# Two gated layers on one core: the first attention's values computed token by token, rearranged through DRAM, and its queries evacuated by ScalarE

## The chip, the cores and the metric

The kernel runs on one core of one Trainium2 chip. The metric is the device time of one execution in microseconds (us), less is better. A core has TensorE (PE; its weight loads are listed as PEld), VectorE (DVE), ScalarE (ACT), GpSimd (POOL), and SyncE (SP), which here issues DMAs.

## The reference, cut to what matters

Two layers follow one another. Each is `x + s * g`, where `s` is an attention and `g` a gated network on the normalised `x`. The first layer's attention works over heads, within each token: for every token the 16 query heads are compared with the 16 key heads of the same token.

```python
def _L0_attn_ref(x, w_qkv, b_qkv, w_out, b_out):
    qkv = x @ w_qkv + b_qkv
    qkv = qkv.reshape(Bq, Lq, NUM_HEADS, 3 * HEAD_DIM)      # 16 heads of 64
    q, k, v = jnp.split(qkv, 3, axis=-1)
    k = k + pos_enc[None, :, None, :]
    attn = jnp.einsum('blhd,blgd->blhg', q, k) / scale
    attn = jax.nn.softmax(attn, axis=-1)
    out = jnp.einsum('blhg,blgd->blhd', attn, v)
    return out.reshape(Bq, Lq, NUM_HEADS * HEAD_DIM) @ w_out + b_out
```

Here x is 2 sequences of 1024 tokens, 128 features wide, in fp32. The rest (the first layer's mixture of 16 experts with its router, the second layer's attention over tokens and its ternary network) is left as it is.

## The kernel before, in words

Each engine runs one instruction stream, written out in order at the end of `two_layers` (lines 2223 to 2409); semaphores tie the streams together. `first_norm` loads and normalises, `head_attention` is the stage of the change, `experts`, `second_attention` and `last_network` follow.

`head_attention` works in 8 blocks of 128 tokens (of both sequences at once) and 16 turns of 64 tokens, two turns to a block. Activations lie feature-major: features on the partitions, tokens along the free axis. In turn `i`, TensorE's stream (`tensor`, line 633) is, in this order:

- `tensor_scores`, two halves (line 558): a query-by-key product for 8 groups of 8 tokens, into banks 2 to 5;
- projection units of the next block (`tensor_project`, line 528): a block has 12 units, 4 of q, 4 of k, 4 of v, and a turn runs 6. A unit is 8 fp32 products into one of banks 0 and 1. It waits until the unit two before it has been evacuated. Turn 0 starts at unit 8, so an even turn runs v, v, v, v, q, q and an odd turn q, q, k, k, k, k. The first two units stand together, the other four alternate with
- the four quarters of `tensor_out` (line 595): the weighted sum for turn `i - 2`, from `vt` (values with (head, token) on the partitions) and `wide` (the probabilities spread over a block-diagonal);
- `tensor_values`, two halves of 4 transposes (line 577), which turn this turn's v into `vt` by way of banks 2 and 3;
- `tensor_turn` (line 586), two transposes of the probabilities of turn `i - 1`; a step of the norm or the router (`f.tensor`); and `tensor_y` (line 615), the output projection of turn `i - 2`.

VectorE masks the scores (`vector_same`, L682), evacuates q and k units (L671, L677, with bias or position added), sums ex (L720) and takes reciprocals, reduces the scores (L691) and takes the top (L731). ScalarE takes exps (L782), evacuates v units with four 128-column instructions each (L762), copies the transposed v into `vt` (L777), the sums (L770), the turned probabilities (L788) and y (L793). GpSimd subtracts the top (L848), spreads the probabilities over `wide` with four instructions for turn `i - 2` (`gpsimd_wide`, L833), scales (L857), and then, in even turns, makes `kb` for the next block (L824), in eight later turns a slice of the experts' weights' parts (L441 to L447). So the spread of turn `i - 2` stands behind the subtraction of turn `i - 1`, which waits for L731. SP only issues the loads of the start (lines 177 to 200), all at once, and waits for nothing. The two score blocks of a turn go through `sm0` and `sm1`; the last turn is written out by hand and interleaved with the experts' first products (lines 2238 to 2259).

An fp32r product takes its operands' rounded parts: the experts' matrices are products hi·hi + lo·hi + hi·lo of such parts (lines 1032 to 1038).

## Time and profile before

| | |
|---|---|
| Time, median of 3 runs | 1138.16 us (1137.54 to 1138.43) |
| The profiled execution, own time | 1136.68 us |
| its span, first to last instruction | 1134.6 us |
| granted TensorE clock, mean | 0.997 |
| head-attention turns (first scores to the experts) | about 20.8 to 232 us of the span |
| DMA in the first 28 us | 219 GB/s, 2 to 3 GB/s after that until the next stage's loads |

A profile's page gives the busy time of each engine, then slices of the span, DMA, the chain of work that ended last, and groups of instructions. The share of busy time says which engine could be the bound; the chain of waits in order of time, and the timeline of a stretch, say what a given turn waited for. A matrix product's recorded duration overlaps its neighbours', so what one costs is read from the distance between starts. One fp32 product appears as two records.

### The profile page before, as it was taken

The numbers are of one execution on the slowest core, as the hardware profiler recorded it, in microseconds if no ns is written. First come the engines' busy times: TensorE is split into PE (matmuls) and PEld (weight loads), VectorE is DVE, ScalarE is ACT, GpSimd is POOL, SyncE is SP. The second block draws the span as 40 slices with busy tenths as digits, with TensorE's granted clock in tenths as the row PEclk, the third lists the DMA queues.
The fourth block names the chain that finished last, engine by engine and source line by source line (L and its number), as shares of the span: only waits on it lengthen the run. The fifth ranks groups of instructions, "written<-read, shape, count | busy, mean of one in ns | idle before, by whom it ended". The sixth has DMA issues, their size and how long they took to land.

```text
span 1134.6 us, 22214 instructions
## 1 busy us (share of the span) xinstructions
PE 1116.5 (98%) x8936; PEld 730.3 (64%) x8936; DVE 847.5 (75%) x1251; ACT 597.8 (53%) x949; POOL 783.8 (69%) x505
## 2 busy tenths in 40 slices
PE   9999999999989999999999999999999999999998
PEld 8899999887765555555454555455455555457886
DVE  5676886657676788878788788878788887896554
ACT  2443444657656555545555555555465455654443
POOL 3666776854436888888987988988988888960000
PEclk9999999999999999999999999999999999999999
DMA  6000000020000000200000000000000000000000
GB/s 219 3 2 2 3 3 3 2 77 1 1 1 1 1 1 26 77 2 1 1 1 1 1 1 2 1 1 1 1 1 1 1 1 1 1 1 10 1 10 19
DMA packets 7686, 13.69 MB, mean 12 GB/s; under 512 B 1809, under 2 KB 5137, under 8 KB 7329
## 3 DMA queue, kind: packets, MB, share of 16 engines
q1 hardware_dynamic: 7264, 12.26, 3.3%
q8 instruction: 72, 1.18, 0.4%
q14 instruction: 30, 0.24, 0.1%
q10 hardware_dynamic: 320, 0.01, 0.0%
HBM read 11.22 MB, written 1.05 MB: 11 GB/s over the span
## 4 chain that ended last, share of the span: by engine, by line
PE 90%; DVE 6%; ACT 2%; issue 2%; POOL 0%; DVEq 0%; ACTq 0%; POOLq 0%
PE o_ps L1547 19%; PE ha_banks L553 7%; PE mx_ps L1502 7%; PE st_ps L1525 5%; PE st_ps L1531 5%; PE st_ps L1528 5%; PE bank L1943 3%; PE bank L1945 3%; PE bank L1944 3%; PE ha_banks L620 3%; PE ha_banks L573 3%; PE mx_ps L1440 3%; PE ha_banks L609 2%; PE pj_ps L1459 2%; PE pj_ps L1451 2%; DVE mx_part L1755 2%
## 5 line engine op out<-in xcount | busy, mean ns | idle before, releaser
L1857 POOL TENSOR_TENSOR acc<-acc,prob 128x1024 f32<-128x1024 f32 x192 | 468.6, 2440 | 63.0 <-ACT prob L1681 52.8
L1681 ACT ACTIVATE prob<-st_ps 128x1024 f32<-128x1024 f32 x256 | 248.5, 1023 | 208.8 <-PE st_ps L1531 208.8
L1547 PE MATMUL o_ps<-prob,v_cur 128*64 128x512 f32 x1024 | 245.6, 599 | 0.0
L1752 DVE TENSOR_REDUCE mx_part<-mx_ps 128x1 f32<-128x512 f32 x258 | 164.8, 666 | 72.4 <-PE mx_ps L1502 72.4
L1547 PEld LDWEIGHTS o_ps<-prob,v_cur 128*64 128x64 f32 x1024 | 68.0, 136 | 96.3 <-issue 77.5
L1755 DVE TENSOR_REDUCE mx_part<-mx_ps 128x2 f32<-128x1024 f32 x79 | 94.9, 1201 | 44.6 <-PE mx_ps L1502 44.6
L1771 DVE RECIPROCAL rden<-rden 128x128 f32<-128x128 f32 x128 | 120.5, 942 | 0.0
L1502 PEld LDWEIGHTS mx_ps<-k_hi,q_hi 64*128 64x128 f32 x416 | 46.7, 183 | 107.2 <-issue 95.5
L1502 PE MATMUL mx_ps<-k_hi,q_hi 64*128 64x512 f32 x416 | 112.3, 457 | 1.5 <-DVE mx_part L1755 1.3
L1531 PE MATMUL st_ps<-q_hi,d_lo 64*128 64x512 f32 x512 | 100.9, 391 | 0.0
L1857 POOL TENSOR_TENSOR acc<-prob 128x1024 f32<-128x1024 f32 x32 | 76.1, 2379 | 29.3 <-PE pj_ps L1436 18.9
L833 POOL TENSOR_TENSOR ha_wide<-ha_pt,ha_own 128x512 f32<-128x512 f32 x64 | 73.7, 1183 | 8.3 <-ACT ha_pt L788 8.3
L1525 PE MATMUL st_ps<-q_hi,d_hi 64*128 64x512 f32 x384 | 75.9, 392 | 0.0
L1528 PE MATMUL st_ps<-q_lo,d_hi 64*128 64x512 f32 x384 | 75.1, 388 | 0.0
L553 PE MATMUL ha_banks<-xn,head_wkv 128*64 128x128 f32 x1024 | 66.0, 274 | 1.6 <-DVE ha_q L671 1.0
L1752 DVE TENSOR_REDUCE mx_part<-pj_ps 128x1 f32<-128x512 f32 x86 | 58.0, 675 | 0.0
L553 PEld LDWEIGHTS ha_banks<-xn,head_wkv 128*64 128x64 f32 x1024 | 55.0, 136 | 4.6 <-DVE ha_q L671 1.4
L1531 PEld LDWEIGHTS st_ps<-q_hi,d_lo 64*128 64x128 f32 x512 | 48.2, 185 | 11.1
L2069 ACT ACTIVATE whole<-bank,cols 128x512 f32<-128x512 f32 x32 | 22.0, 688 | 62.1 <-PE bank L1945 60.1
L682 DVE TENSOR_TENSOR ha_sm<-ha_banks,ha_same 128x1024 f32<-128x1024 f32 x32 | 37.6, 1216 | 19.9 <-PE ha_banks L573 19.8
L762 ACT ACTIVATE ha_v<-ha_banks,ha_head_bv 128x128 f32<-128x128 f32 x128 | 35.6, 375 | 24.6 <-PE ha_banks L553 24.6
L1645 ACT ACTIVATE rden<-pj_ps 128x512 f32<-128x512 f32 x32 | 19.1, 598 | 53.9 <-PE pj_ps L1451 53.9
(404 smaller groups left out, 2319.3 us busy)
## 6 DMA issues: line engine op xcount, KB each, us to landing
h_w<-in_h SPq DMA_DIRECT2D x2, 1024.0 KB, 7.8
w_raw<-in_w SPq DMA_DIRECT2D x8, 192.0 KB, 3.6
head_wkv<-in_wkv SPq DMA_DIRECT2D x2, 512.0 KB, 6.3
m_w<-in_m SPq DMA_DIRECT2D x3, 256.0 KB, 2.9
out<-fin SPq DMA_DIRECT2D x3, 256.0 KB, 2.2
sel_raw<-in_sel SPq DMA_DIRECT2D x1, 576.0 KB, 10.1
head_wq<-in_wq SPq DMA_DIRECT2D x1, 512.0 KB, 4.4
x<-in_x SPq DMA_DIRECT2D x2, 256.0 KB, 7.8
```

Source lines behind the costliest of these rows:

```text
L553: mm = pe.matmul(pj_ps[n % 2][rows(seq), j, :], lhs, xn[:, seq * HALVES + b // TT, at_token:at_token + BLK], start=True, stop=True, skip_g ...
L833: d = pool.tensor_tensor(wide[r][:, seq, :, :, :], t.unsqueeze(3).to_broadcast([P, G // 2, HEADS, GROUPS]), own[:, :].unsqueeze(1).unsquee ...
L1502: mm = pe.matmul(to[h], q_hi[q % 2][rows(h), tile(i)], k_hi[q % 2][rows(h), half_of(keys)], start=True, stop=True)
L1525: pe.matmul(st[:, h, :], upper[rows(h), :], qh[rows(h), half_of(half)], start=False, stop=False, skip_group_check=True)
L1528: pe.matmul(st[:, h, :], upper[rows(h), :], ql[rows(h), half_of(half)], start=False, stop=False, skip_group_check=True)
L1531: mm = pe.matmul(st[:, h, :], dl[rows(h), tile(j)], qh[rows(h), half_of(half)], start=False, stop=True, skip_group_check=True)
L1547: mm = pe.matmul(o_ps[rows(h), :], v_cur[:, m % 2, j, rows(h)], prob[:, (16 * m + slot) % RING, h, :], start=(j == 0), stop=(j == KT - 1), ...
L1681: act.activation(prob[:, n % RING, :, :], st_ps[:, slot % 2, :, :], ACT.Exp, scale=SCALE).then_inc(s_exp, 1)
L1752: dve.reduce_max(mx_part[:, h, i, keys:keys + 1], maxima_banks(q, n)[h], AX_X).then_inc(s_mxr, 1)
L1755: dve.reduce_max(mx_part[:, :, i, keys:keys + 1], both, AX_X).then_inc(s_mxr, 1)
L1771: dve.reciprocal(part, part).then_inc(s_rcp, 1)
L1857: pool.tensor_tensor(total, old, new, ALU.add).then_inc(s_acc, 1)
```

## The change: what it does

- **Values.** A v unit is now one sequence and eight heads: 128 tokens on the output's partitions, 512 columns (head, dimension). It is three fp32r products: hi·hi, hi·lo, lo·hi, of parts of the tokens (`xv_hi` by ScalarE, `xv_lo` by GpSimd, one block at a time) and of the weights (`wv_hi` by ScalarE, the low part by GpSimd into the place of the weights, once at the start). The v units keep their places in the order.
- **Evacuation.** VectorE evacuates v, adding a bias row that is broadcast to all partitions; q goes to ScalarE, four instructions for each unit. k stays with VectorE but is written group by group, and both its inputs are now read with a step of 16 elements. VectorE evacuates the third v unit before its first reduction of an even turn, and the fourth between the two.
- **The rearrangement.** The 16 transposes of a block and their copies go. SP, once a block's four v units are out, stores v (1 MB) to DRAM, waits for the store, and loads each turn's `vt` (512 KB) in pieces of 512 bytes, behind a wait for the weighted sums of two turns before. `tensor_out` waits for that load.
- **Order of rows.** Tokens and heads are (group, head) instead of (head, group) on the partitions of `vt`; `prob` is written with another inner order, a second mask tile `mask_g` is loaded, and y is written in the new token order.
- **The start.** The bias row is first gathered, DRAM to DRAM, in 1024 pieces of 4 bytes; SP waits for it before it issues the broadcast and all the loads behind it (positions, the second half of x, `wo`, the router's and the experts' weights). The masks' loads are issued between the gather and the wait.
- **The end.** The experts' second gate product stands one step earlier; its wait is for the last masked scores.

The diff, cut to its core:

```diff
@@ -28,7 +28,7 @@
-HEAD_W = {"wo": (PAIRS, P), "bq": (2, PAIRS), "bk": (HEADS,), "bv": (HEADS,), "pos": (LEN,), "mask_h": (P,)}
+HEAD_W = {"wo": (PAIRS, P), "bq": (2, PAIRS), "bk": (HEADS,), "pos": (LEN,), "mask_h": (P,), "mask_g": (P,)}
...
@@ -184,9 +185,13 @@
+        sp.dma_start(w.bv_row, a["bkv0"][HD:P, :].rearrange("n h -> h n"), allow_slow_non_contiguous=True)\
+            .then_inc(s_row, 16)
-        for seq in range(SEQS):
-            sp.dma_start(w.bv[HD * seq:HD * seq + HD, :], a["bkv0"][HD:P, :]).then_inc(s_bv, 16)
+        sp.dma_start(w.mask_g[:, :], a["mask"]).then_inc(s_mask, 16)
+        sp.wait_ge(s_row, 16)
+        sp.dma_start(w.bv[:, :, :], w.bv_row.unsqueeze(0).to_broadcast([P, HEADS, HD])).then_inc(s_bv, 16)
...
@@ -478,12 +491,13 @@
-    q, k = zip(*((room.sb(f"q{i}", [P, BLK // G, HEADS, G]), room.sb(f"k{i}", [P, HEADS, BLK])) for i in range(2)))
-    v = room.sb("v", [P, BLK // TURN, G, HEADS, GROUPS])
+    q, k = zip(*((room.sb(f"q{i}", [P, BLK // G, HEADS, G]), room.sb(f"k{i}", [P, BLK // G, HEADS, G])) for i in range(2)))
+    v = room.sb("v", [P, HEADS, SEQS, HD])
...
-    sc, ex, prob = ([room.sb(f"{n}{i}", [P, SEQS, HEADS, GROUPS]) for i in range(2)] for n in ("sc", "ex", "prob"))
+    sc, ex = ([room.sb(f"{n}{i}", [P, SEQS, HEADS, GROUPS]) for i in range(2)] for n in ("sc", "ex"))
+    prob = [room.sb(f"prob{i}", [P, SEQS, GROUPS, HEADS]) for i in range(2)]
...
@@ -513,6 +528,32 @@
+    def grouped(t):
+        return t.rearrange("r h (t g) -> r h g t", t=G)
...
+    def value_unit(u):
+        return u % SEQS, slice((u - 2 * QU) // SEQS * PAIRS, (u - 2 * QU) // SEQS * PAIRS + PAIRS)
...
+    def over_rows(t):
+        return t[:, :, :, :].rearrange("r s g h -> r s h g")
...
@@ -529,37 +570,48 @@
-            pe.wait_ge(f.s_cur, {0: 1, 1: 2, TT: CHUNKS}[b])
+            wait_tokens(pe, b)
...
-            if u_was < 2 * QU:
-                pe.wait_ge(s_qk, b_was * 2 * QU + u_was + 1)
+            if u_was < QU:
+                pe.wait_ge(s_q, b_was * QU + u_was + 1)
+            elif u_was < 2 * QU:
+                pe.wait_ge(s_k, b_was * QU + u_was - QU + 1)
...
+        if u >= 2 * QU:
+            if u == 2 * QU:
+                pe.wait_ge(s_xvlo, b + 1)
+                if b == 0:
+                    pe.wait_ge(s_wvlo, 1)
+            seq, heads = value_unit(u)
+            hi, lo = (t[:, b % 2, seq, :] for t in (w.xv_hi, w.xv_lo))
+            to = banks[:, n % 2, :]
+            pe.matmul(to, hi, w.wv_hi[:, heads, :], start=True, stop=False)
+            pe.matmul(to, hi, w.wkv_lo[:, heads, HD:P], start=False, stop=False)
+            pe.matmul(to, lo, w.wv_hi[:, heads, :], start=False, stop=True).then_inc(s_pj, 1)
+            return
...
-            pe.wait_ge(s_qk, (i // 2 + 1) * 2 * QU)
+            pe.wait_ge(s_q, (i // 2 + 1) * QU)
+            pe.wait_ge(s_k, (i // 2 + 1) * QU)
         if half == 0 and i >= 1:
-            pe.wait_ge(s_vtc, 2 * i)
+            pe.wait_ge(s_mul, 2 * i - 1)
...
-                               k[i // 2 % 2][rows(seq), :, of * G:of * G + G], start=True, stop=True)
+                               k[i // 2 % 2][rows(seq), of, :, :], start=True, stop=True)
...
-    def tensor_values(pe, i, half):
-        if half == 0:
-            if i % 2 == 0:
-                pe.wait_ge(s_vo, (i // 2 + 1) * QU)
-            pe.wait_ge(s_mul, 2 * i + 1)
-        for t in range(G // 2):
-            mm = pe.transpose(x_ps[half][:, tile(t)], v[:, i % 2, half * G // 2 + t, :, :], c.ident[:, :])
-        mm.then_inc(s_vt, 1)
...
-            pe.wait_ge(s_vtc, 2 * n + r + 1)
+            if r == 0:
+                pe.wait_ge(s_vt[n % 2], 16 * (n // 2 + 1))
...
-        tensor_values(pe, i, 0)
-        tensor_values(pe, i, 1)
...
@@ -658,24 +700,29 @@
-        if u >= 2 * QU:
+        if u < QU:
...
-        if u < QU:
-            dve.wait_ge(s_pj, n + 1)
-            bias = w.bq[:, :, :].rearrange("r o p -> r (o p)")[:, heads].unsqueeze(2).unsqueeze(3)
-            d = dve.tensor_tensor(q[b % 2][:, :, heads, :].rearrange("r g h t -> r h g t"),
-                                  pj_ps[n % 2][:, :, :].rearrange("r h (g t) -> r h g t", t=G),
-                                  bias.to_broadcast([P, UNIT, BLK // G, G]), ALU.add)
...
-            d = dve.tensor_tensor(k[b % 2][:, heads, :], pj_ps[n % 2][:, :, :], kb[:, heads, :], ALU.add)
-        d.then_inc(s_qk, 1)
+            dve.tensor_tensor(k[b % 2][:, :, heads, :].rearrange("r g h t -> r h g t"), grouped(pj_ps[n % 2]),
+                              grouped(kb[:, heads, :]), ALU.add).then_inc(s_k, 1)
+            return
+        seq, heads = value_unit(u)
+        if n == 2 * QU:
+            dve.wait_ge(f.s_bv, 16)
+        if u == 2 * QU and b >= 1:
+            dve.wait_ge(s_vst, 16 * b)
+        dve.wait_ge(s_pj, n + 1)
+        dve.tensor_tensor(v[:, heads, seq, :], banks[:, n % 2, :].rearrange("r (h n) -> r h n", n=HD), w.bv[:, heads, :],
+                          ALU.add).then_inc(s_vo, 1)
...
-        dve.wait_ge(f.s_mask, 16)
+        dve.wait_ge(f.s_mask, 32)
-        dve.tensor_scalar(own[:, :], w.mask_h[:, 0:P:HEADS], 0.0, None, ALU.is_ge).then_inc(s_same, 1)
+        dve.tensor_scalar(own[:, :], w.mask_g[:, 0:P:HEADS], 0.0, None, ALU.is_ge).then_inc(s_same, 1)
...
-        for b, u in units(i, (2, 3, 4) if i % 2 else ()):
+        for b, u in units(i, (2, 3, 4) if i % 2 else (2,)):
...
-        for b, u in units(i, (5,) if i % 2 else ()):
+        for b, u in units(i, (5,) if i % 2 else (3,)):
...
-        for b, u in units(i, () if i % 2 else (4, 5)):
-            vector_project(dve, b, u)
...
@@ -746,22 +790,45 @@
...
-        if u < 2 * QU:
+        if u >= QU:
...
+        if n == 0:
+            act.wait_ge(f.s_bq, 16 * 2 * SEQS)
...
+        bias = w.bq[:, :, :].rearrange("r o p -> r (o p)")
-            h = u % QU * UNIT + j
-            d = act.activation(v[:, :, :, h, :], pj_ps[n % 2][:, j, :].rearrange("r (o g t) -> r o t g", t=G, g=GROUPS),
-                               ACT.Identity, bias=w.bv[:, h:h + 1])
-        d.then_inc(s_vo, 1)
+            h = u * UNIT + j
+            d = act.activation(q[b % 2][:, :, h, :], pj_ps[n % 2][:, j, :].rearrange("r (t g) -> r g t", t=G),
+                               ACT.Identity, bias=bias[:, h:h + 1])
+        d.then_inc(s_q, 1)
+    def scalar_tokens(act, b):
+        wait_tokens(act, b)
+        if b >= 2:
+            act.wait_ge(s_pj, (b - 1) * UNITS)
+        act.activation(w.xv_hi[:, b % 2, :, :], tokens_of(b), ACT.Copy).then_inc(s_xvhi, 1)
+    def scalar_begin(act):
+        scalar_tokens(act, 0)
+        scalar_project(act, 0, 0)
+        f.scalar_first_square(act, 1)
+        scalar_project(act, 0, 1)
+        scalar_project(act, 0, 2)
+        f.scalar_first_root(act, 1)
+        scalar_project(act, 0, 3)
+        wait_heads(act)
+        act.activation(w.wv_hi[:, :, :], w.wkv[:, :, HD:P], ACT.Copy).then_inc(s_wvhi, 1)
...
-    def scalar_values(act, i, half):
-        act.wait_ge(s_vt, 2 * i + half + 1)
-        act.activation(vt[i % 2][:, half * G // 2:half * G // 2 + G // 2, :].rearrange("r t n -> r (t n)"), x_ps[half],
-                       ACT.Copy).then_inc(s_vtc, 1)
...
@@ -789,28 +849,27 @@
-        tokens = c.y[:, :].rearrange("r (s b o g t) -> r s b o g t", s=SEQS, t=G, g=GROUPS, o=BLK // TURN)
-        act.activation(tokens[:, :, n // 2, n % 2, :, :].rearrange("r s g t -> r t s g"),
+        tokens = c.y[:, :].rearrange("r (s b t o g) -> r s b o t g", s=SEQS, t=G, g=GROUPS, o=BLK // TURN)
+        act.activation(tokens[:, :, n // 2, n % 2, :, :].rearrange("r s t g -> r t s g"),
...
-        for b, u in units(i, (0, 1, 2, 3)):
+        for b, u in units(i, (0, 1) if i % 2 else ()):
             scalar_project(act, b, u)
+        if i % 2 and i // 2 + 1 < BLOCKS:
+            scalar_tokens(act, i // 2 + 1)
-        for b, u in units(i, (4, 5)):
+            scalar_out(act, i - 2, 1)
+        for b, u in units(i, () if i % 2 else (4,)):
             scalar_project(act, b, u)
-        if i >= 2:
-            scalar_out(act, i - 2, 1)
-        scalar_values(act, i, 0)
-        scalar_values(act, i, 1)
         if i >= 1:
             scalar_turned(act, i - 1)
+        for b, u in units(i, () if i % 2 else (5,)):
+            scalar_project(act, b, u)
...
@@ -835,10 +894,35 @@
+    def gpsimd_tokens(pool, b):
+        pool.wait_ge(s_xvhi, b + 1)
+        if b >= 2:
+            pool.wait_ge(s_pj, (b - 1) * UNITS)
+        pool.tensor_tensor(w.xv_lo[:, b % 2, :, :], tokens_of(b), w.xv_hi[:, b % 2, :, :].bitcast(F32), ALU.subtract)\
+            .then_inc(s_xvlo, 1)
+    def sync(sp):
+        for b in range(BLOCKS):
+            sp.wait_ge(s_vo, (b + 1) * QU)
+            sp.dma_start(w.v_rows[b], v[:, :, :, :].rearrange("r h s n -> r (h s n)")).then_inc(s_vst, 16)
+            sp.wait_ge(s_vst, 16 * (b + 1))
+            by_turn = w.v_rows[b].rearrange("(t o g) (h n) -> o (g h) t n", t=G, g=GROUPS, n=SEQS * HD)
+            for o_turn in range(BLK // TURN):
+                n = b * (BLK // TURN) + o_turn
+                if n >= 2:
+                    sp.wait_ge(s_o, 2 * (n - 2) + 2)
+                sp.dma_start(vt[n % 2][:, :, :], by_turn[o_turn]).then_inc(s_vt[n % 2], 16)
...
+        gpsimd_tokens(pool, 0)
+        pool.wait_ge(s_wvhi, 1)
+        pool.tensor_tensor(w.wkv_lo[:, :, HD:P], w.wkv[:, :, HD:P], w.wv_hi[:, :, :].bitcast(F32), ALU.subtract).then_inc(s_wvlo, 1)
...
-            pool.tensor_tensor(prob[n % 2][:, :, :, :], ex[n % 2][:, :, :, :], over_heads(rtotal[n % 2]), ALU.mult)\
+            pool.tensor_tensor(over_rows(prob[n % 2]), ex[n % 2][:, :, :, :], over_heads(rtotal[n % 2]), ALU.mult)\
+        if i % 2 and i // 2 + 1 < BLOCKS:
+            gpsimd_tokens(pool, i // 2 + 1)
...
-            pe.wait_ge(head.s_vtc, 2 * head.TURNS)
+            pe.wait_ge(head.s_mul, 2 * head.TURNS)
...
@@ -2169,6 +2256,13 @@
+        w.wv_hi = room.sb("head_wv_hi", [P, HEADS, HD], F32R)
+        w.wkv_lo = Region(nc, XR + 4 * KB).sb("head_wkv_lo", [P, HEADS, P], F32R)
+        w.bv = room.sb("head_bv", [P, HEADS, HD])
+        w.xv_hi, w.xv_lo = (room.sb(n, [P, 2, SEQS, P], F32R) for n in ("head_xv_hi", "head_xv_lo"))
+        w.v_rows = nc.dram_tensor("v_rows", (LEN // P, P, SEQS * HEADS * HD), F32, kind="Internal").ap()
+        w.bv_row = nc.dram_tensor("bv_row", (HEADS, HD), F32, kind="Internal").ap()
...
+                head.sync(sp)
...
@@ -2240,12 +2335,10 @@
-                head.tensor_values(pe, TURNS - 1, 0)
-                head.tensor_values(pe, TURNS - 1, 1)
+                e.tensor_gates(pe, 1)
...
-                e.tensor_gates(pe, 1)
...
+                head.scalar_begin(act)
```

## Rows read from the trace of the kernel before

**Rows 1.** The page's first part: busy time of each engine, share, instructions.

```profile
PE 1116.5 (98%) x8936; PEld 730.3 (64%) x8936; DVE 847.5 (75%) x1251; ACT 597.8 (53%) x949; POOL 783.8 (69%) x505
```

**Rows 2.** Chain of waits in order of time, 0 to 330: start, duration (us), work.

```profile
110.45 1.99 PE ha_banks L573 x32
...
122.74 1.99 PE ha_banks L573 x32
...
135.19 1.99 PE ha_banks L573 x32
```

**Rows 3.** Timeline, 107 to 134, weight loads: start, duration, engine, line, out<-in, count.

```profile
119.64 0.86 PEld L583 LDWEIGHTS ha_banks<-ident,ha_v 128*128 128x128 f32 x8 [0.17 <-issue]
...
120.46 0.25 PEld L592 LDWEIGHTS ha_banks<-ident,ha_prob 128*128 128x128 f32 x2
...
122.67 1.86 PEld L573 LDWEIGHTS ha_banks<-ha_k,ha_q 64*128 64x128 f32 x32
...
124.65 1.73 PEld L553 LDWEIGHTS ha_banks<-xn,head_wkv 128*64 128x64 f32 x32
...
126.34 0.60 PEld L609 LDWEIGHTS ha_banks<-ha_wide,ha_vt 128*64 128x64 f32 x16
...
127.05 0.85 PEld L553 LDWEIGHTS ha_banks<-xn,head_wkv 128*64 128x64 f32 x16
...
128.38 0.86 PEld L553 LDWEIGHTS ha_banks<-xn,head_wkv 128*64 128x64 f32 x16
```

**Rows 4.** Timeline, 198 to 250, matrix products, where fp32r and fp32 products meet.

```profile
213.07 0.49 PE L1036 MATMUL g_ps<-xm_hi,wg_hi 128*128 128x512 f32 x1
...
213.40 0.39 PE L1037 MATMUL g_ps<-xm_hi,wg_lo 128*128 128x512 f32 x1
...
214.66 1.15 PE L609 MATMUL ha_banks<-ha_wide,ha_vt 128*64 128x64 f32 x32
```

**Rows 5.** Timeline, 107 to 134, VectorE and GpSimd at a turn's change.

```profile
122.06 0.61 DVE L731 TENSOR_REDUCE ha_top<-ha_sc 128x16 f32<-128x256 f32 x1
...
123.44 4.72 POOL L833 TENSOR_TENSOR ha_wide<-ha_pt,ha_own 128x512 f32<-128x512 f32 x4
```

**Rows 6.** Groups by line and form: busy us, mean ns, idle before them.

```profile
L682 DVE TENSOR_TENSOR ha_sm<-ha_banks,ha_same 128x1024 f32<-128x1024 f32 x32 | 37.6, 1216 | 19.9 <-PE ha_banks L573 19.8
...
L677 DVE TENSOR_TENSOR ha_k<-ha_banks,ha_kb 128x512 f32<-128x512 f32 x32 | 21.6, 675 | 9.4 <-PE ha_banks L553 9.2
...
L731 DVE TENSOR_REDUCE ha_top<-ha_sc 128x16 f32<-128x256 f32 x16 | 10.0, 622 | 0.6
...
L377 DVE TENSOR_REDUCE ha_top<-ha_lg 128x16 f32<-128x256 f32 x1 | 0.4, 407 | 0.0
...
L762 ACT ACTIVATE ha_v<-ha_banks,ha_head_bv 128x128 f32<-128x128 f32 x128 | 35.6, 375 | 24.6 <-PE ha_banks L553 24.6
...
L1857 POOL TENSOR_TENSOR acc<-acc,prob 128x1024 f32<-128x1024 f32 x192 | 468.6, 2440 | 63.0 <-ACT prob L1681 52.8
```

**Rows 7.** DMA: queue (packets, MB, share of 16 engines); issues (KB, us to landing).

```profile
q1 hardware_dynamic: 7264, 12.26, 3.3%
...
head_wq<-in_wq SPq DMA_DIRECT2D x1, 512.0 KB, 4.4
...
out<-fin SPq DMA_DIRECT2D x3, 256.0 KB, 2.2
...
ha_head_bq<-in_bq ACTq DMA_DIRECT2D x4, 2.0 KB, 3.2
```

**Rows 8.** Timeline, first turns: the masks, and the first weighted sum.

```profile
20.67 0.25 DVE L696 TENSOR_SCALAR ha_same<-ha_head_mask_h 128x128 f32<-128x128 f32 x1
...
45.11 0.69 PE L609 MATMUL ha_banks<-ha_wide,ha_vt 128*64 128x64 f32 x16 [0.60 <-issue]
```

**Rows 9.** Timeline, 198 to 250: the weighted sum of turn 14.

```profile
220.54 1.15 PE L609 MATMUL ha_banks<-ha_wide,ha_vt 128*64 128x64 f32 x32
```

71 lines of the change are left out of this document (38 added, 33 removed).

## The prediction

> **What bounds the kernel now.** I read the page's busy times first. TensorE is busy 98% of the span [rows 1], so only what leaves TensorE's stream, or holds it up, moves the end. The chain of waits in order of time then shows the stage that is changed: scores follow scores at 110.45, 122.74 and 135.19 us, so an odd turn takes 12.29 us and an even one 12.45 [rows 2]. Last the timeline of the even turn that begins at 122.67 [rows 3] splits it: scores 1.98 (to 124.65), the first two v units 1.69 (to 126.34), a unit and a quarter of the weighted sum together 1.33 (127.05 to 128.38), the eight transposes 0.82 (119.64 to 120.46, in the turn before), and the turned probabilities with the output projection 2.21 (to 122.67). Of the 0.71 between 126.34 and 127.05 a quarter needs 0.53; the rest, 0.18, is a wait for a v evacuation. TensorE is back to back; the others run behind it. What matters is how close.
>
> **What the change removes.** The transposes go: 0.82 us a turn, 16 turns, 13.1 us at most [rows 3]. The 32 copies to `vt` go from ScalarE, which wasn't late.
>
> **What the new product costs.** In a later stretch six fp32r products of 512 columns stand between fp32 ones: 213.07 to 214.66, 1.59 us; the first takes 0.33, because it follows another kind of product, the other five 0.25 each with the change back at the end [rows 4]. So the first pair of v units (six products) costs 1.59 for 1.69 now, and a lone unit of three 0.33 + 2 × 0.25 = 0.83 for 1.69 / 2 = 0.85. Three fast products in place of eight slow ones save 0.1 us a block: nothing.
>
> **The steady even turn, walked.** Time 0 is its scores' start.
> - The odd turn before is 0.82 shorter. Its last VectorE step, the top, doesn't follow: it hangs on the last k unit, which TensorE makes before the transposes stood. Now the top ends at 122.06 + 0.61 = 122.67, at time 0 [rows 5]; then at 0.82.
> - GpSimd's spread began 0.77 after that and takes 4.72, its first half 2.36 [rows 5]: ready at 0.82 + 0.77 + 2.36 = 3.95. TensorE wants it at 1.98 + 1.59 = 3.57. A new stall of 0.38. It exists because the cover was the transposes.
> - VectorE has masked both halves (2 × 1.22 [rows 6]) by about 3.6 (its start, 1.2, is the end of the first half of the scores), and takes v units in 0.68 each (as a k unit now, 675 ns [rows 6]): first out at 4.3, TensorE wants its bank at 3.95 + 0.53 = 4.5. Third and fourth: out at about 6.6 and 8.5 (behind the sums and the first reduction), wanted at about 7.3 and 8.7. No stall, but 0.2 of slack.
> - ScalarE's q units cost four instructions, as v units did, at 375 ns [rows 6], and start later in an even turn; their banks are wanted only in the next turn. In an odd turn it does them first thing after the exps. Hidden by the copies that left. Rounding tokens and subtracting them (256 elements) are small, at places where ScalarE and GpSimd wait.
> - So an even turn changes by −0.82 − 0.10 − 0.18 + 0.38 = −0.7, an odd one by −0.82. Turns 3 to 14 are six of each: **−9.1 us**.
>
> **The last turn.** Its transposes stood where TensorE waited for the probabilities of VectorE; the moved gate product covers the same wait. Saved: 0. But the last `vt` load is due early, see below.
>
> **The DRAM trip.** Store 1 MB: a 256 KB store landed in 2.2 us [rows 7], so between 2.2 and 8.8; load 512 KB: `head_wq` took 4.4 [rows 7]; in 512-byte pieces it may be more. 3.3% of 16 engines' 1134.6 us over 7264 packets is 0.08 us a packet [rows 7], and 64 pieces an engine are 5.3 us and landing. I take 6 and 6, with 1.2 for two issues: v complete at 8.5, `vt` at about 22. It is due at 11.75 + 11.47 + 3.95 = 27.2. Hidden, with 5 us of slack; without that cover each us too late is paid in each of 7 blocks. For the last block no projection lies between: turn 14's sum ran at 220.54 [rows 9], 22.1 after its scores, and would now be due at 21.4. Ready at 8.5 + 2.2 + 4.4 + 1.2 = 16.3 at best, 24 at worst: 0 to 2.6 us, I take 0.5.
>
> **The start.** SP now waits for the gather of 1024 pieces, 64 an engine: at 0.08 each, 5 us [rows 7], behind the weights in the same queues. All later loads slide by as much; then VectorE's first v evacuation waits for the broadcast row, and GpSimd must make the weights' low part (1024 columns, 2.4 us by [rows 6]) before the first v unit. I put 1.6 us on the first two turns, which uses up their two lots of transposes. The first round trip is queued behind the weights: turn 2's sum, at 45.11 now [rows 8], may wait 0 to 4 us; I take 1.3, of which 0.82 is paid by turn 2's transposes: +0.5.
>
> **Sum.** −9.1 + 0.5 + 0.5 = −8.1: the profiled execution's 1136.68 becomes 1128.6. The median is 1.48 above it, so 1130.1; I say **1130**. By the ends of the unknown costs, 1128.5 to 1135.
>
> **Rivals.**
> - *The step of 16.* VectorE's k evacuation reads two operands with long steps. The same reduction of 256 elements takes 622 ns with a step of 8 elements (L731) and 407 without (L377) [rows 6]: 0.84 ns an element, 0.43 us a k unit, four in each odd turn. Against it: L696 reads 128 elements with a step of 16 in 0.25 us [rows 8], no longer than its size asks. If it bites, two of the four delays reach the top (the others hide in the 1.3 between units), so the spread starts 0.85 later, the stall is 1.2, and everything VectorE does in the even turn slides: even turns end 0.2 above now instead of 0.7 below. 1130 + 6 × 0.9 = **1135.5**. The Trainium skill says so too (SBUF — State Buffer, Door 1: The DMA port swizzle): accesses that cross to a new 16-byte line pay a penalty, so fp32 strides above 4 aren't free; by that rule this rival holds, and L731 agrees with it while L696 doesn't.
> - *The scores run faster.* 16 score products take 1.98, 16 products of a unit pair 1.69 [rows 3]. If the 0.29 comes from k's scattered reading, contiguous k gives it back, 14 times: **1126**. For it: the same columns. Against: scores also follow another kind of product, as in [rows 4].
> - *The gather holds SP* (slower). Four tiny loads of 2 KB took 3.2 us with at most 4 pieces an engine [rows 7], so a piece could cost up to 0.8 us when it isn't overlapped. The masks stand behind the gather and are used at 20.67 [rows 8]. The queues are free at about 14; above 0.1 us a piece the masks are late, us for us. At 0.3: 14 + 19 = 33, 12 late, **1142**. For it: each piece is a DRAM read and write of its own. Against: 0.08 is the mean of packets of 1.7 KB.
> - *The round trip is late in each block* (slower). It decides from 18.7 us after v is complete. If 512-byte pieces cost twice the mean packet and the store 8.8, `vt` comes at about 30, 3 late, 7 times: **1150**.
> - *The change doesn't do what it says:* no such case here; the transposes are gone from the stream.
>
> **How the numbers follow.** Forecast 0.45, step of 16 0.25, faster scores 0.12, gather 0.10, late round trip 0.08. A measurement of this kernel can tell 0.2% (2.3 us) from no change: below 1135.9 is faster, above 1140.4 slower. The forecast and the faster scores are faster (0.57), the step of 16 lies on the edge, half to each (0.12 and 0.13); of the two slower rivals 0.02 end within. Faster 0.69, same 0.15, slower 0.16. The range takes in the first three cases and the near part of the gather: 1125 to 1140.
>
> **What would show it.** Right: scores 11.5 us apart in odd turns and about 11.7 in even ones; a stall of 0.4 before an even turn's first sum, released by GpSimd's spread; v units 1.59 a pair; 675 ns for L677's successor; `vt`'s load released 4 or 5 us before its use. Wrong: a k evacuation near 1.1 us (step of 16); scores below 1.9; VectorE's masks or the sums waiting for a DMA; a stall of TensorE on a v unit's evacuation, which my slack of 0.2 us doesn't exclude.

## The result, and the profile after

The changed kernel takes 1141.68 us (median; 1140.52 to 1142.95) against 1138.43 for the kernel before on the same chip (1136.99 to 1141.55): a ratio of 1.0025, 95% interval 1.0014 to 1.0037. It is slower by about 3 us where 8 us of gain were forecast, and lies outside the range of 1125 to 1140. The profiled execution took 1140.92 us, 4.24 above the one of before, with a span of 1139.1, 4.5 above. It is one execution of nine, and its mean granted clock was 0.996, that of the eight others 0.992 or 0.993. The traces of e2 and e4, whose other turns are as long to 0.2 us save turns 5 and 6, have 0.992, and there turn 10 takes 18.04 and 17.74 instead of 16.74. So most executions lose more to the clock than the trace read here.

The page's first part of the changed kernel answers to [rows 1]. TensorE is busy 8.0 us less, and the span is 4.5 longer: TensorE now waits.

```profile
PE 1108.5 (97%) x8392; PEld 709.3 (62%) x8392; DVE 858.0 (75%) x1251; ACT 583.4 (51%) x926; POOL 792.0 (70%) x514
```

Where the time went is read from the starts of the turns' scores, in the chain of waits in order of time (start, duration, work), which answers to [rows 2] (in a timeline the same start can stand 0.07 earlier):

```profile
23.65 1.18 PE ha_banks L625 x16
...
44.51 2.06 PE ha_banks L625 x32
...
112.67 1.99 PE ha_banks L625 x32
...
124.19 1.99 PE ha_banks L625 x32
...
127.78 1.25 issue
...
137.15 1.99 PE ha_banks L625 x32
...
153.49 2.34 DVE ha_sm L729 x2
155.83 0.61 DVE ha_v L724
156.48 0.70 PE ha_banks L594
...
165.42 1.99 PE ha_banks L625 x32
...
213.26 1.99 PE ha_banks L625 x32
```

The turns' lengths in the two timelines, from one start of the scores to the next, and in the three experiments that matter most (us):

| turn | before | after | e5 | e7 | e9 |
|---|---|---|---|---|---|
| first scores start at | 20.81 | 23.65 | 24.43 | 20.75 | 21.62 |
| 0 and 1 together | 19.75 | 20.86 | 19.91 | 19.29 | 19.37 |
| 2 | 14.88 | 14.65 | 14.64 | 14.64 | 14.64 |
| 5 and 6 together | 28.33 | 28.30 | 29.89 | 28.49 | 29.89 |
| 7, 9 (odd) | 12.29 | 11.52 | 11.52 | 11.53 | 11.52 |
| 4, 8, 12 (even), mean | 12.75 | 12.82 | 12.13 | 12.23 | 12.11 |
| 10 | 12.73 | 16.74 | 16.13 | 14.07 | 12.10 |
| scores of turn 15 start at | 210.00 | 213.19 | 211.36 | 203.89 | 204.04 |
| span | 1134.6 | 1139.1 | 1136.4 | 1130.2 | 1129.4 |

Three things read at once. Turns 7, 9, 11 and 13 are 0.77 shorter, close to the forecast. Even turns gain nothing on the whole: 4 and 12 are 0.17 and 0.13 shorter, 8 is 0.51 longer. Two places lose much: the start, 3.95 by the scores of turn 2, and turn 10, 4.01.

The groups by line and form of the first 240 us, which answer to [rows 6]: k's read-out takes 1032 ns where it took 675; q, v, the masks and the maximum take what they were expected to.

```profile
L653 PE MATMUL ha_banks<-ha_wide,ha_vt 128*64 128x64 f32 x1024 | 41.0, 225 | 6.7 <-issue 6.6
...
L729 DVE TENSOR_TENSOR ha_sm<-ha_banks,ha_same 128x1024 f32<-128x1024 f32 x32 | 37.6, 1214 | 16.0 <-PE ha_banks L625 15.9
...
L810 ACT ACTIVATE ha_q<-ha_banks,ha_head_bq 128x128 f32<-128x128 f32 x128 | 35.8, 384 | 26.2 <-PE ha_banks L605 26.2
...
L714 DVE TENSOR_TENSOR ha_k<-ha_banks,ha_kb 128x512 f32<-128x512 f32 x32 | 32.9, 1032 | 13.8 <-PE ha_banks L605 13.8
...
L724 DVE TENSOR_TENSOR ha_v<-ha_banks,head_bv 128x512 f32<-128x512 f32 x32 | 20.9, 674 | 2.0 <-PE ha_banks L596 2.0
...
L777 DVE TENSOR_REDUCE ha_top<-ha_sc 128x16 f32<-128x256 f32 x16 | 9.9, 622 | 0.6
```

The timeline of the even turn that starts at 124.12, VectorE, GpSimd and TensorE, which answers to [rows 5]:

```profile
125.07 0.62 DVE L777 TENSOR_REDUCE ha_top<-ha_sc 128x16 f32<-128x256 f32 x1
...
126.70 2.34 DVE L729 TENSOR_TENSOR ha_sm<-ha_banks,ha_same 128x1024 f32<-128x1024 f32 x2
...
126.45 4.73 POOL L892 TENSOR_TENSOR ha_wide<-ha_pt,ha_own 128x512 f32<-128x512 f32 x4
...
129.03 0.69 PE L653 MATMUL ha_banks<-ha_wide,ha_vt 128*64 128x64 f32 x16 [1.25 <-issue]
```

The maximum ends at 125.69, 1.57 after the scores' start (forecast: 0.82), GpSimd's spread starts at 2.33 and has its first half done about 2.4 later, and TensorE, ready at 127.78, stands still for 1.25 until 129.03. Over the stage the waits before weighted sums come to 6.6 us in 7 places; before they were 0.6 in one. One of the seven, 1.10, stands in the last turn, where the moved gate product no longer fills it.

Turn 10, the timeline of VectorE and TensorE. The router's steps of turn 9 (L412 to L419) hold VectorE until 153.5, then come both masks and only then the v units; TensorE's third v unit needs a bank whose read-out stands behind all of it, and waits 2.41:

```profile
151.22 1.05 DVE L417 TENSOR_SCALAR ha_mask<-ha_rep 128x256 f32<-128x256 f32 x1
152.30 1.26 DVE L419 TENSOR_TENSOR ha_wt<-ha_mask,ha_pr 128x256 f32<-128x256 f32 x1
153.49 2.34 DVE L729 TENSOR_TENSOR ha_sm<-ha_banks,ha_same 128x1024 f32<-128x1024 f32 x2
155.75 1.27 DVE L724 TENSOR_TENSOR ha_v<-ha_banks,head_bv 128x512 f32<-128x512 f32 x2
...
156.48 0.70 PE L594 MATMUL ha_banks<-head_wv_hi,head_xv_hi 128*128 128x512 f32 x1 [2.41 <-DVE ha_v L724]
156.97 0.63 PE L595 MATMUL ha_banks<-head_wkv_lo,head_xv_hi 128*128 128x512 f32 x1
```

Before the change the same router steps stood in the same place (timeline of VectorE, kernel before), but no read-out that TensorE waits for came behind the masks:

```profile
148.46 1.03 DVE L407 TENSOR_SCALAR ha_mask<-ha_rep 128x256 f32<-128x256 f32 x1
149.53 1.27 DVE L409 TENSOR_TENSOR ha_wt<-ha_mask,ha_pr 128x256 f32<-128x256 f32 x1
150.72 2.34 DVE L682 TENSOR_TENSOR ha_sm<-ha_banks,ha_same 128x1024 f32<-128x1024 f32 x2
```

The third v unit's products then take up to 0.70 and 0.63 where others take 0.50 and 0.40. The table by stretch of the changed kernel shows the clock behind it (busy us of PE, PEld, DVE, ACT, POOL, each with its count; granted clock; DMA share; GB/s). In 152 to 156 TensorE worked 0.95 us of 4; behind that its clock is 0.58, that is, mostly the 1.2 GHz level instead of 2.4:

```profile
12.00:16.00 4.00, 3.98 (x58) 3.72 (x56) 0.37 (x2) 3.38 (x12) 0.53 (x1) 1.00 0.02 5
16.00:20.00 4.00, 2.77 (x40) 2.22 (x38) 1.60 (x2) 1.77 (x5) 2.15 (x1) 1.00 0.00 0
...
98.00:102.00 4.00, 4.00 (x32) 3.78 (x32) 0.05 (x1) 0.58 (x2) 4.00 (x5) 0.57 0.00 0
...
152.00:156.00 4.00, 0.95 (x18) 0.58 (x16) 3.97 (x5) 0.00 (x0) 3.71 (x4) 1.00 0.02 4
156.00:160.00 4.00, 3.52 (x21) 2.50 (x22) 3.62 (x6) 0.53 (x1) 2.02 (x3) 0.58 0.00 0
```

The same table has the start: from 12 to 20 us the DMA engines move next to nothing. The masks' loads have landed by 12.3, and SyncE queues nothing else: it waits for the gather, and issues the next load at 19.14. In the table of the kernel before, the same two stretches moved 262 and 386 GB/s:

```profile
12.00:16.00 4.00, 3.98 (x58) 3.64 (x54) 2.15 (x4) 0.97 (x2) 0.52 (x1) 1.00 0.98 262
16.00:20.00 4.00, 4.00 (x63) 3.49 (x61) 3.06 (x5) 0.00 (x0) 0.00 (x0) 1.00 1.02 386
```

The changed kernel's table also has a second drop of the clock, 0.57 in 98 to 102, with TensorE busy all the time.

The round trip, from the DMA issues (KB, us from issue to landing), which answers to [rows 7]: 3.9 and 4.0, and no wait for it shows in a steady turn.

```profile
v_rows<-ha_v SPq DMA_DIRECT2D x8, 1024.0 KB, 3.9
ha_vt<-v_rows SPq DMA_DIRECT2D x16, 512.0 KB, 4.0
```

### The profile page after: what moved, and what is told of

It is laid out like the page before. It is cut to its first block, busy times and chain, and to the rows that moved or that the text cites. A ratio compares the mean times of both kernels' runs of the same rounds, so it can differ in the third digit from the quotient of the medians.

```text
span 1139.1 us, 21143 instructions
## 1 busy us (share of the span) xinstructions
PE 1108.5 (97%) x8392; PEld 709.3 (62%) x8392; DVE 858.0 (75%) x1251; ACT 583.4 (51%) x926; POOL 792.0 (70%) x514
## 4 chain that ended last, share of the span: by engine, by line
PE 89%; DVE 7%; issue 2%; ACT 2%; POOL 0%; DVEq 0%; ACTq 0%; POOLq 0%
PE o_ps L1634 19%; PE mx_ps L1589 7%; PE st_ps L1612 5%; PE st_ps L1615 5%; PE st_ps L1618 5%; PE ha_banks L605 5%; PE bank L2030 3%; PE bank L2031 3%; PE bank L2032 3%; PE ha_banks L653 3%; PE mx_ps L1527 3%; PE ha_banks L664 2%; PE pj_ps L1546 2%; PE ha_banks L625 2%; PE pj_ps L1538 2%
## 5 line engine op out<-in xcount | busy, mean ns | idle before, releaser
L837 ACT ACTIVATE ha_o<-ha_banks 128x512 f32<-128x512 f32 x32 | 19.2, 599 | 69.7 <-PE ha_banks L653 69.7
L810 ACT ACTIVATE ha_q<-ha_banks,ha_head_bq 128x128 f32<-128x128 f32 x128 | 35.8, 384 | 26.2 <-PE ha_banks L605 26.2
L653 PE MATMUL ha_banks<-ha_wide,ha_vt 128*64 128x64 f32 x1024 | 41.0, 225 | 6.7 <-issue 6.6
```

The costliest lines, as they stand in the source:

```text
L653: mm = pe.matmul(o_ps[r][rows(odd), t, seq, :], vt[n % 2][:, r * G // 2 + t, rows(seq)], wide[r][:, seq, t, PAIRS * odd:PAIRS * odd + PAIR ...
```

## The experiments

All ratios are to the kernel before, run in turns on the same chip; the changed kernel stands at 1.0025. The experiments ran on four chips (e1 to e4, e5 to e8, e9, e10 and e11), so two of them are compared by their ratios. The profile shows one execution of each, and some of the effects below are smaller than what one differs from the next: the first k product starts anywhere from 14.60 to 15.85 in the thirteen traces.

**e1: k laid out plainly, scores read with a step.**

```diff
-    q, k = zip(*((room.sb(f"q{i}", [P, BLK // G, HEADS, G]), room.sb(f"k{i}", [P, BLK // G, HEADS, G])) for i in range(2)))
+    q, k = zip(*((room.sb(f"q{i}", [P, BLK // G, HEADS, G]), room.sb(f"k{i}", [P, HEADS, BLK])) for i in range(2)))
-                               k[i // 2 % 2][rows(seq), of, :, :], start=True, stop=True)
+                               k[i // 2 % 2][rows(seq), :, of:BLK:BLK // G], start=True, stop=True)
-            dve.tensor_tensor(k[b % 2][:, :, heads, :].rearrange("r g h t -> r h g t"), grouped(pj_ps[n % 2]),
-                              grouped(kb[:, heads, :]), ALU.add).then_inc(s_k, 1)
+            dve.tensor_tensor(k[b % 2][:, heads, :], pj_ps[n % 2][:, :, :], kb[:, heads, :], ALU.add).then_inc(s_k, 1)
```

> The changed kernel with k laid out as before the change: VectorE takes it out with plain runs, and the scores read the eight tokens of a group 16 apart. Result unchanged. Theory A (VectorE's 1.03 us for each k unit makes the maximum of an odd turn late, the spread weights late, and TensorE waits 1.25 us before the first weighted sum of each even turn): a k unit takes 0.68 us, the waits named issue before the sums shrink from 6.6 us to under 2, the scores stay at 2.0 us a turn, each even turn from turn 2 on is 0.7 to 1.2 us shorter, and the kernel is 5 to 8 us faster than the changed one, about 1133 to 1136. Rival B (the read-out is not on the path and the gain of TensorE is lost elsewhere): the k units are shorter, but the waits before the sums stay and the time is within 1 us of 1141.7. Rival C (the step only moves): the scores' own products get longer by more than 0.3 us a turn, and the kernel is as slow as the changed one or slower.

Measured: 1154.28 us, ratio 1.0139 (1.0110 to 1.0167). Rival C. The k units took 688 ns, as A and C say, but the score products, in the groups by line, grew from a mean of 283 to 396 ns, 1.7 us a turn:

```profile
L625 PE MATMUL ha_banks<-ha_k,ha_q 64*128 64x128 f32 x512 | 59.8, 396 | 0.4 <-issue 0.4
```

A step costs TensorE's moving operand too, and there it is on the path. The run says nothing on A: turns of 13.2 us hide any wait.

**e2: the step on the writing side.** VectorE reads in runs and writes element by element, 128 elements apart, since the groups of `k` lie 16 heads times 8 tokens apart.

```diff
-            dve.tensor_tensor(k[b % 2][:, :, heads, :].rearrange("r g h t -> r h g t"), grouped(pj_ps[n % 2]),
-                              grouped(kb[:, heads, :]), ALU.add).then_inc(s_k, 1)
+            dve.tensor_tensor(k[b % 2][:, :, heads, :].rearrange("r g h t -> r h t g"),
+                              pj_ps[n % 2][:, :, :].rearrange("r h (t g) -> r h t g", t=G),
+                              kb[:, heads, :].rearrange("r h (t g) -> r h t g", t=G), ALU.add).then_inc(s_k, 1)
```

> The changed kernel with one edit: VectorE walks a k unit in the order in which it lies in the banks, so it reads in runs and writes with a step. Layouts and result unchanged. Theory A with reading as what costs: 0.68 us for a unit and the same gain as in e1_k_read_stepped, 1133 to 1136. If a step costs the same on the writing side, a unit stays at 1.0 us and the time at 1141 to 1142.

Measured: 1140.98 us, ratio 1.0018 (1.0007 to 1.0029). The second case: a unit takes 1061 ns. The read step of 16 elements and the write step of 128 cost VectorE about the same.

**e3: the first v unit between the masks.**

```diff
         vector_same(dve, i, 0)
+        for b, u in units(i, (0,)):
+            vector_project(dve, b, u)
         vector_same(dve, i, 1)
-        for b, u in units(i, (0, 1)):
+        for b, u in units(i, (1,)):
             vector_project(dve, b, u)
```

> The changed kernel with one edit: VectorE takes out the first v unit of an even turn between its two mask multiplications instead of behind both. Theory D (turn 10 lost 4.1 us because that unit, now VectorE's, stood behind the router's steps of turn 9 and behind both masks, so that TensorE stood still from 154 to 156.5 and its clock fell): the turn that starts at 148.6 takes 13.5 to 14.5 us instead of 16.8, the clock stays at 1.00 in 156 to 160, and the kernel is 2.5 to 3.5 us faster than the changed one, 1138 to 1139. Rival E (the weighted sums would have waited for the spread weights anyway, these being late by the router's steps too): the turn stays over 16 us and the time within 1 us of 1141.7.

Measured: 1138.50 us, ratio 1.0004 (0.9992 to 1.0015): 2.4 us less than the changed kernel by the ratios, just short of theory D's 2.5 to 3.5, and less than half of it in D's place. Turn 10 fell only from 16.74 to 15.62; TensorE still waited 1.28 for a v unit, behind 1.15 for the spread weights, and the clock still fell (0.76 in 152 to 156, 0.81 in 156 to 160). Another 0.55 came in turn 0, to which the edit applies too, and 1.0 at the start, where VectorE's first k unit began at 17.38 instead of 18.40; no instruction ahead of it was changed, and 0.86 of it is already in the unit's product (14.60 for 15.46). So D is half shown here. The 1.15 for the spread weights isn't the router's: the maximum stands ahead of the router's steps and ends 1.58 after the scores' start, as late as in turn 8 (1.57), and the wait is the even turns' ordinary one, which shrinks to 0.43 once k is read plainly (e7).

**e4: the loads ahead of SyncE's wait.**

```diff
-        sp.wait_ge(s_row, 16)
-        sp.dma_start(w.bv[:, :, :], w.bv_row.unsqueeze(0).to_broadcast([P, HEADS, HD])).then_inc(s_bv, 16)
         load_positions(sp, a, w, s_pos)
         for p in (2, 3):
             i = ORDER[p]
             sp.dma_start(x[:, i, :], a["x"][:, i * CH:i * CH + CH]).then_inc(s_x[p], 16)
+        sp.wait_ge(s_row, 16)
+        sp.dma_start(w.bv[:, :, :], w.bv_row.unsqueeze(0).to_broadcast([P, HEADS, HD])).then_inc(s_bv, 16)
```

> The changed kernel with one edit: SyncE issues the positions and the two later chunks of x before it waits for the gathered bias row, not behind it. Theory F (the start lost its 3 to 4 us on VectorE and ScalarE: the read-out of k and of q and the square root behind two q units): the first four score starts stay within 0.5 us of 23.65, 33.47, 44.51 and 59.16, though GpSimd's keys of the second block start some 3 us or more before 27.3. The time stays within 1 us of 1141.7. Rival G (SyncE's wait of 9.9 us makes the start late): score start 2 comes at 41 to 43 and the kernel is 2 to 3 us faster.

Measured: 1143.22 us, ratio 1.0037 (1.0024 to 1.0049). Both theories fail: the first scores come later, at 25.30, and VectorE's first k unit at 20.06. The table by stretch (columns as above) shows the new loads moving at about a sixth of the rate of the kernel before, then a ninth, while the engines count as busy for a share of 1.19 and 0.64:

```profile
12.00:16.00 4.00, 3.98 (x60) 3.72 (x58) 0.55 (x2) 3.20 (x11) 0.89 (x2) 1.00 1.19 43
16.00:20.00 4.00, 3.01 (x36) 2.19 (x32) 0.00 (x0) 1.95 (x5) 1.97 (x1) 1.00 0.64 41
```

So moving SyncE's wait doesn't help; e6 tests whether it is the gather itself.

**e5: the regrouping moved into the store.** Which eight tokens form a group is free, as long as q, k, v and the result agree. So q, k and the result go back to eight tokens in a row, and v's rows are put in the order of the step of 16 by the store to DRAM.

```diff
-                               k[i // 2 % 2][rows(seq), of, :, :], start=True, stop=True)
+                               k[i // 2 % 2][rows(seq), :, of * G:of * G + G], start=True, stop=True)
-            dve.tensor_tensor(k[b % 2][:, :, heads, :].rearrange("r g h t -> r h g t"), grouped(pj_ps[n % 2]),
-                              grouped(kb[:, heads, :]), ALU.add).then_inc(s_k, 1)
+            dve.tensor_tensor(k[b % 2][:, heads, :], pj_ps[n % 2][:, :, :], kb[:, heads, :], ALU.add).then_inc(s_k, 1)
...
-            sp.dma_start(w.v_rows[b], v[:, :, :, :].rearrange("r h s n -> r (h s n)")).then_inc(s_vst, 16)
+            sp.dma_start(w.v_rows[b].rearrange("(t e) m -> e t m", t=G), v[:, :, :, :].rearrange("r h s n -> r (h s n)")).then_inc(s_vst, 16)
```

> The changed kernel with the regrouping of tokens moved from the read-outs of q and k into the store of v: a group is eight tokens in a row as before the change, VectorE and ScalarE take k and q out with plain runs, the scores read k in runs of eight, and the store writes the token rows of v to DRAM in the order of the step of 16, so that the load back is unchanged. Result unchanged. Theory A (the k read-out of 1.03 us makes the maximum, the spread weights and so the even turns' sums late): a k unit takes 0.68 us, the scores 2.0 us a turn, the waits named issue before the sums fall from 6.6 us to under 2, even turns are 0.7 to 1.2 us shorter, odd ones unchanged at 11.5, turn 10 gains 1.4 more, and the kernel is 6 to 9 us faster than the changed one: 1132 to 1136. Rival B (the gain of TensorE in even turns is lost to something else, such as GpSimd's 4.7 us for the spread weights): k at 0.68 but the waits stay, 1140 to 1142. A store that writes with a step may take longer than the 3.9 us; up to about 8 us it changes nothing.

Measured: 1136.06 us, ratio 0.9983 (0.9974 to 0.9993). Theory A in its mechanism, at the low end of its sizes: k units 689 ns, turns 4, 8 and 12 shorter by 0.66 to 0.72, turn 1 by 1.0, waits before the sums 3.6 instead of 6.6 us (under 2 expected). In the even turn that starts at 125.00 (timeline) the maximum ends 0.88 after the scores' start, and 0.57 of waiting are left:

```profile
125.27 0.61 DVE L776 TENSOR_REDUCE ha_top<-ha_sc 128x16 f32<-128x256 f32 x1
...
129.23 0.69 PE L653 MATMUL ha_banks<-ha_wide,ha_vt 128*64 128x64 f32 x16 [0.57 <-issue]
```

The store took 6.2 us instead of 3.9, and no wait for it shows. The gain over the changed kernel is 5 us and not 6 to 9. Turn 10 gained 0.6, not 1.4, and the even turns the least of what was expected. In the profiled execution turns 5 and 6 together also lost 1.6 to the clock (0.78 in 94 to 98, 0.50 in 98 to 102), but it is the slowest of the twelve, 2.2 above their median, so this doesn't explain the median.

**e6: no gather.**

```diff
-        sp.dma_start(w.bv_row, a["bkv0"][HD:P, :].rearrange("n h -> h n"), allow_slow_non_contiguous=True)\
-            .then_inc(s_row, 16)
+        sp.dma_start(w.bv_read[:, :, :], a["bkv0"][HD:P, :].unsqueeze(0).to_broadcast([P, HD, HEADS])).then_inc(s_row, 16)
-        sp.wait_ge(s_row, 16)
-        sp.dma_start(w.bv[:, :, :], w.bv_row.unsqueeze(0).to_broadcast([P, HEADS, HD])).then_inc(s_bv, 16)
...
+        act.wait_ge(f.s_row, 16)
+        act.activation(w.bv[:, :, :], w.bv_read[:, :, :].rearrange("p n h -> p h n"), ACT.Copy).then_inc(f.s_bv, 1)
```

> The changed kernel without the gather: the 4 KB of v's bias are broadcast to all rows as they lie in memory, one load without a wait on SyncE, and ScalarE rearranges them once, after the high parts of v's weights (about 1 us). Result unchanged. Theory G2 (not SyncE's wait but the gather of 1024 single values holds the DMA engines, which move nearly nothing between 12 and 20 us, and with them the start, VectorE's first k unit among it, which began 1.9 us after its product was done): the DMA engines move 200 GB/s or more there, the first k unit starts within 0.2 us of its product's end (about 16.6), the first scores come 1.5 to 2 us earlier, near 22, scores of turn 2 near 42.5, and the kernel is 1.5 to 3 us faster than the changed one, 1138.5 to 1140. Theory F (the start is late by VectorE's and ScalarE's own work): VectorE's first k unit stays at 18.4 and the time at 1141 to 1142.

Measured: 1140.16 us, ratio 1.0013 (1.0003 to 1.0024). G2: VectorE's first k unit starts at 16.69, the first scores come at 22.01, and the engines move what they moved before:

```profile
12.00:16.00 4.00, 3.98 (x60) 3.72 (x58) 0.43 (x2) 3.33 (x11) 1.10 (x2) 1.00 1.04 277
16.00:20.00 4.00, 3.65 (x56) 3.06 (x52) 3.31 (x4) 3.74 (x6) 2.09 (x1) 1.00 1.04 372
```

The first scores gained 1.64, and VectorE's first k unit starts 0.12 after its product's end; turns 5 and 6 together lost 1.6 to the clock in this profile.

**e7: e3, e5 and e6 together.**

> The three edits together: the groups by the store (e5), no gather (e6), the first v unit of an even turn between the masks (e3). Result unchanged. If theories A, D and G2 hold and add up: turn 10 near 13, even turns 11.7 to 12.2, first scores near 21.5, and the kernel 10 to 13 us faster than the changed one, 1128.5 to 1132, faster than the kernel before by 0.6 to 0.9%. If the gains are the same idle time counted three times: 1134 to 1136.

Measured: 1131.92 us, ratio 0.9951 (0.9936 to 0.9966), faster than both kernels; and the gains add up, as far as intervals of 0.1% each can say: 0.21% (e3), 0.42% (e5) and 0.12% (e6) make 0.75%, measured 0.74%. The first scores are back at 20.75. Counted from the start of the first k product (15.12 before, 15.46 in the changed kernel, 15.53 in e6, 14.96 in e7) they come after 5.69 before, 8.19 in the changed kernel, 6.48 in e6 and 5.79 in e7. So of the 2.84 lost, the gather held 1.7 and the stepped k units 0.7; 0.3 lay ahead of the k products, within what one trace differs from another. Turn 10 takes 14.07 at a clock of 1.00.

**e8: what TensorE's time was worth before the change.**

```diff
-        for t in range(G // 2):
+        for t in range(1):
             mm = pe.transpose(x_ps[half][:, tile(t)], v[:, i % 2, half * G // 2 + t, :, :], c.ident[:, :])
```

> The kernel before with one edit: of the eight transposes of v in each turn TensorE does two, and ScalarE copies as before; three quarters of the rearranged v are left out, so the output isn't the reference's. It asks what TensorE's 0.82 us a turn are worth in the kernel before. Theory T (TensorE sets all turns): 14 turns by 0.7 to 0.8 us, 9 to 11 us, 1127 to 1129. Theory H (TensorE sets the odd turns; in the even ones the spread weights or ScalarE come next after a few tenths): odd turns 0.7 to 0.8 shorter, even ones 0.2 to 0.4, together 6 to 8 us, 1130 to 1132.

Measured: 1129.58 us, ratio 0.9923 (0.9911 to 0.9935), 7.7 us less by the medians. The number lies between the two ranges, the pattern is T's: odd turns (7, 9) are 0.65 shorter and even ones (8, 10) 0.56 and 0.64. T was mispriced by me: six of eight transposes are 0.82 × 6 / 8 = 0.62 a turn, 8.1 us in 13 turns. In the kernel before TensorE did set all turns alike, and nearly all it was given came through. It is the changed kernel's own additions that took it back.

**e9: v taken out by ScalarE.** As e5, with v's bias added to the result as one column instead of to v.

```diff
-        dve.tensor_tensor(v[:, heads, seq, :], banks[:, n % 2, :].rearrange("r (h n) -> r h n", n=HD), w.bv[:, heads, :],
-                          ALU.add).then_inc(s_vo, 1)
...
+            act.activation(v[:, heads, seq, :], banks[:, n % 2, :].rearrange("r (h n) -> r h n", n=HD), ACT.Copy)\
+               .then_inc(s_vo, 1)
...
+            for p in range(PAIRS):
+                mm = pe.matmul(y_ps[:, 0, 0:1], w.wo[:, p, :], w.bv_col[:, p:p + 1], start=p == 0, stop=p == PAIRS - 1)
...
-                       ACT.Copy).then_inc(s_yc, 1)
+                       ACT.Identity, bias=w.yb[:, :]).then_inc(s_yc, 1)
```

> As e5_groups_by_the_store, and ScalarE takes out v, as before the change: one plain copy for each unit, since v's bias is left out of v and added to the block's result as one column, w.wo times the bias column, worked out in turn 1 (eight products of one column; the weights of a token sum to one). The gather and the broadcast of the bias row go. Result unchanged. VectorE loses four v units of 0.67 us in each even turn, ScalarE gains them. Theory D2 (turn 10 is long because VectorE's v read-outs stand behind the router's steps; the rest of the loss at the start was the gather and the stepped k read-out): turn 10 takes 12.0 to 12.6 us against 14.07 in e7_three_together, no wait for a v read-out over 0.5 us, the clock stays at 1.00 in turn 10, the first scores come near 20.7, and the kernel is 1 to 3 us faster than e7_three_together: 1129 to 1131. Theory W (in even turns the spread weights, GpSimd's 4.8 us behind the maximum, set the first sum whoever takes out v): turn 10 still over 13.5 us, the time 1131 to 1133.

Measured: 1128.63 us, ratio 0.9918 (0.9903 to 0.9933), by the ratios 3.8 us less than e7, more than the 1 to 3 expected. D2: turn 10 takes 12.10, with no wait for a v read-out, though VectorE runs the same router steps; before the first sum 0.45 is left (timeline of TensorE):

```profile
145.53 2.06 PE L624 MATMUL ha_banks<-ha_k,ha_q 64*128 64x128 f32 x32
...
149.62 0.69 PE L654 MATMUL ha_banks<-ha_wide,ha_vt 128*64 128x64 f32 x16 [0.45 <-issue]
```

The first scores came at 21.62, not 20.7; the 0.9 lies ahead of the first k product, which started at 15.85 (14.96 in e7), and from there on the two are alike, 5.77 and 5.79.

**e10 and e11: the clock in turn 5.** e10 is the changed kernel and e11 is e9, each with the router's products of turn 5 moved out of their one piece. In the changed kernel (timeline of TensorE) the router's 32 products of 16 columns run in one piece, and what follows is slow: the output projection takes 2.73 instead of 1.95, the scores 2.95 instead of 2.06.

```profile
93.94 3.64 PE L283 MATMUL ha_banks<-ha_rw,xn 128*128 128x16 f32 x32
97.44 2.73 PE L664 MATMUL ha_banks<-ha_o,ha_head_wo 128*128 128x128 f32 x16
100.09 2.95 PE L625 MATMUL ha_banks<-ha_k,ha_q 64*128 64x128 f32 x32
```

```diff
         for p in range(PAIRS):
             mm = pe.matmul(y_ps, w.wo[:, p, :], o[:, :, :, p, :], start=p == 0, stop=p == PAIRS - 1)
+            if n + 2 == f.LOGITS:
+                f.tensor_logits(pe, (2 * p, 2 * p + 1))
...
```

> The changed kernel with one edit: the router's logits of turn 5 (L283, 32 instructions' worth of products of 16 columns, 3.64 us in one piece, after which the output projection took 2.73 us and the next scores 2.95 instead of 1.95 and 2.06, at a granted clock of 0.57 in 98 to 102) are issued between the eight pairs of the output projection, two tiles behind each. Result unchanged. Theory N (the stretch of narrow products pulls the clock down): the clock in 94 to 102 stays at 1.00, turn 5 and turn 6 are 0.7 and 0.8 us shorter, and the kernel is 1.5 us faster than the changed one, near 1140. Rival M (the clock falls whenever those 3.6 us come, mixed or not): turns 5 and 6 stay at 15.8 and 12.5 or get longer, 1141 to 1143.

> e9_v_taken_out_by_scalar with the same mixing. In e9's profile turn 5 took 17.72 us with a clock of 0.50 in 94 to 98, against 15.84 in e7_three_together. Theory N: turn 5 takes 15.0 to 15.3, the clock stays at 1.00, and the kernel is 2 to 3 us faster than e9: 1125.5 to 1127. Rival M: no change, 1128 to 1130.

Measured: e10 1140.08 us, ratio 1.0013 (1.0001 to 1.0025); e11 1128.37, ratio 0.9911 (0.9897 to 0.9925), the fastest version here, not to be told apart from e9. Both profiles go theory N's way: turn 5 takes 15.00 and 15.01, turns 5 and 6 together 26.60 and 26.58 against 28.30 and 29.89, and the clock holds. The table of e10:

```profile
94.00:98.00 4.00, 4.00 (x40) 3.83 (x37) 3.93 (x5) 0.47 (x2) 0.00 (x0) 1.00 0.47 131
98.00:102.00 4.00, 4.00 (x51) 3.85 (x51) 1.33 (x2) 0.58 (x2) 3.96 (x4) 1.00 0.01 4
```

N isn't proven by it. In nine of the eleven traces with the piece in one the clock falls somewhere in 90 to 102; in the kernel before and in e1 it doesn't, and e1 has neither the transposes nor a break: L283 takes 3.64 from 98.72, and the clock is 1.00 from 98 to 106. The medians don't decide it: e10's 1.0013 against the changed kernel's 1.0025 lies within the two intervals, and e11 missed its 1125.5 to 1127. In e11 the profiled execution is 3.1 us shorter than e9's, the median only 0.3; how often the clock falls in turn 5 of an execution of e9 that wasn't profiled I can't say. Nor is the clock saved for good: in e10 it was 0.72 in 152 to 156 and 0.50 in 156 to 160, and turn 10 took 17.50.

## Why the prediction was wrong, step by step

By spans, −8.1 was forecast and +4.5 came: 12.6 us to account for.

| step | forecast | measured | missed |
|---|---|---|---|
| start and turns 0 to 2 | +0.5 | +3.72 | 3.2 |
| even turns 4, 6, 8, 12, 14 | −3.5 | −0.10 | 3.4 |
| turn 10 | −0.7 | +4.01 | 4.7 |
| odd turns 3 to 13 | −4.9 | −4.44 | 0.5 |
| turn 15 and what follows | +0.5 | +1.3 | 0.8 |

- **Odd turns: right.** 0.77 for 0.82, in turns 7, 9, 11 and 13. Turn 5 is only 0.08 shorter at a clock of 0.57 (e10: 0.87 at 1.00), which no step of mine had, and turn 3 is 1.30 shorter, which wasn't looked into. That the six together come within 0.5 of the forecast is partly luck.
- **v's products save nothing: right, and slightly too good.** A pair took 1.67 (126.11 to 127.78) for 1.59, though its starts lie as in [rows 4]: the 0.08 is the end of its last product, which shows because a standstill follows. A lone unit took 0.90 for 0.83, a quarter of the sum next to it 0.61 to 0.66 for 0.53. The meetings of fp32r and fp32 products cost a little more than I took: over a pair, two units and the two quarters beside them 0.08 + 0.13 + 0.07 + 0.08 + 0.07 = 0.43 us a turn that I hadn't priced.
- **The even turn: the step that failed is the top that ends "then at 0.82", which leaves L677's successor at 675 ns.** A k unit took 1032 ns, the top ended at 1.57, and the new stall was 1.25 where the sum has 0.38. The rival of the step of 16 had the price (0.43 forecast, 0.36 measured), the way (two of four delays reach the maximum: 1.57 − 0.82 = 0.75 measured) and the stall (1.2 forecast, 1.25 measured). With 12.45 − 0.82 − 0.10 − 0.18 = 11.35 for the work, 0.43 for the meetings and 1.25 of stall, the turn at 124.12 should take 13.0 and took 12.96. Turn 8 is the worst of the even turns, though: in turn 12 the stall was 0.66, and turns 4 and 12 lost little or nothing. I gave this rival 0.25 because L696 read 128 elements with the same step at no visible cost [rows 8]; a single operand of 128 elements was the wrong row to trust against L731's 0.84 ns an element. e5 shows the cause: without the step the stall is 0.57. Even where this rival was right it was no full answer: it forecast 1135.5, and the start and turn 10 are the rest. The Trainium skill (SBUF — State Buffer, Door 1: The DMA port swizzle) says that each access that crosses to a new 16-byte line pays a penalty, so that fp32 can be stepped over by 4 elements at most for free; by that rule the rival should have been the forecast, and VectorE's 1032 against 675 ns agrees. The page speaks of accesses, and e2's 1061 ns says that writes are among them. Its section is on SBUF, though, and one of the two stepped operands lies in a bank; no run steps only one of them.
- **Turn 10: the step that failed is "first out at 4.3", a walk of a turn without the router.** The stretch I walked had no router steps of 3.4 us on VectorE ahead of the masks. Before, the same steps stood there and did no harm, because v was ScalarE's: I costed v's read-out by its duration on its new engine, and didn't ask what else is queued there. e3 moved one unit and got 1.1, e7 removed the k delay too and got to 14.07, e9 took v off VectorE and got to 12.10: 4.64 in all, the miss. About 0.7 of it is the k delay (the wait before the first sum is 1.12 here and 0.45 in e9). An estimate from two traces puts 0.9 on the lower clock behind the standstill: from the third v unit to the next scores it took 8.87 at 0.58 and 8.02 in e7 at 1.00.
- **The start: right that the gather would cost, wrong in how.** I priced 1024 pieces at the mean time of a packet, 0.08 us, and let SyncE's wait carry the cost. The row was issued at 7.23 and had landed by 19.14, and loads queued behind it got through at 43 and 41 GB/s (e4) where they move 277 and 372 without it (e6). The rival "gather holds SP" had the place but put the cost on late masks; the masks weren't late for their load. The k units' step cost 0.7 more in the same stretch (e6 to e7), and 1.0 in turn 1, which I had left out of the start altogether.
- **The DRAM trip: right and too careful.** 3.9 and 4.0 for 6 and 6. The trip stayed hidden, also with e5's store of 6.2.
- **The last turn: +0.5 forecast, 0.5 measured,** by the start of the experts' second rounding on ScalarE behind the last scores' start (20.6 before, 21.1 after). That the number fits is luck: I expected it from the load, which was issued at 214.27, took 4.0 and wasn't waited for. TensorE waits 0.37 for VectorE's probabilities (0.18 before), and VectorE's difference and probabilities took 1.22 and 1.17 for 0.68 and 0.94; why isn't known, and no run tested it. The other 0.8 of the table's last row came behind the stage: from the scores of turn 15 to the end it is 924.6 before, 925.9 after and 925.0 to 926.3 in e5, e7 and e9, whose code there is the same, and I didn't look into it.

## What to carry to other kernels

When work moves to another engine, list everything that is queued on that engine in every turn where it will run, the odd jobs too, and not in a typical turn: the steps of a router that were harmless cost 4 us once TensorE's banks stood behind them. When a layout has to be permuted, pay for it where there is slack: against e5, which has it in the store to DRAM where it was hidden, the same step of 16 cost 18 us in TensorE's operand (e1) and 5 us on VectorE (the changed kernel). And don't send single 4-byte values through DMA queues that others need.

## What the hardware showed that I had not expected

- A gather of 1024 values of 4 bytes slowed all loads queued behind it: in 12 to 20 us they moved 43 and 41 GB/s (e4), 277 and 372 without it (e6). VectorE's first k unit, which waits for none of these loads, began 1.9 us after its product ended in the changed kernel, 0.9 to 3.4 in the seven traces with the gather, and 0.1 in the four changed ones without it. Why is open; the fetch of its instructions is a candidate that no row here shows. The Trainium skill (DMA: Bandwidth & Descriptors, Why small descriptors are slow (HBM only)) names a fixed cost for each piece, which agrees in direction with the 11.9 us from issue to the end of SyncE's wait for 4 KB.
- TensorE's clock fell to the 1.2 GHz level while its records show it busy without a gap: 32 products of 16 columns took 3.64 us and the granted clock behind them was 0.57; with the same products spread among products of 128 columns it stayed at 1.00 in turn 5 (e10, e11). The piece alone doesn't decide it: in the kernel before, with eight transposes close ahead of it, and in e1, with none, it was followed by 1.00; in e8, with two, by 0.60. The Trainium skill (TensorE: Matmul & The Clock Gate, Part 1) says the clock follows how busy the engine has been; in 98 to 102 the clock was 0.57 with TensorE's records at 4.00 of 4 us before and in it, so the profile's busy time doesn't foretell it here.
- A step of 16 fp32 elements costs each engine differently: VectorE 0.36 us on 512 elements of two operands (and 0.39 when it writes with a step of 128 instead, e2); TensorE's moving operand of 128 columns 0.11 us a product (e1); ScalarE nothing, 384 ns stepped against 386 plain (e9).
